# Splitting the aggregation of mixing weights, adding bias on TensorE, and moving two mixes into the first projection

## The reference, cut to what matters

```python
# x: (32, 64, 1024) f32, cond: (32, 128)
h = gelu(cond @ W0 + b0); h = gelu(h @ W1 + b1)
att = softmax(h @ W2 + b2)                       # (32, 8)
agg_w = einsum('bk,koi->boi', att, weight)       # (32, 64, 64)
z = einsum('boi,bih->boh', agg_w, x) + (att @ bias_k)[:, :, None]
# causal self-attention over each batch's 64 rows, 32 heads of 32, with an adapter prefix of 10
x = x + attention(z, w_attn, w_proj, adapter_wte, gating)
x = x + ffn(grouped_conv(x) + cond @ c_weight.T + fside)   # base matmul, router, top-2 LoRA
```

## Time and profile before

| | |
|---|---|
| median of 3 runs | 1165.27 us (1162.61 to 1166.54) |
| the profiled execution | 1160.39 us |
| its span, first to last instruction | 1158.6 us |
| TensorE (PE) busy | 1141.3 us, 99% |
| VectorE (DVE) busy | 926.9 us, 80% |
| ScalarE (ACT) busy | 442.2 us, 38% |

### The profile page before, as it was taken

One profiled execution on the slowest core, in us unless ns is written; L12 is line 12 of the kernel. 1 busy time (PEld: TensorE's weight loads), 2 busy tenths in 40 slices (PEclk: granted clock), 3 DMA queues, 4 the chain that ended last, 5 costly groups with the idle time before them and its releaser, 6 DMA issues.

```text
span 1158.6 us, 19585 instructions
## 1 busy us (share of the span) xinstructions
PE 1141.3 (99%) x7595; PEld 964.7 (83%) x7595; DVE 926.9 (80%) x1742; ACT 442.2 (38%) x815; POOL 55.2 (5%) x25
## 2 busy tenths in 40 slices
PE   6999999999999999999999999999999999999998
PEld 5988888888888888888888888878888888888887
DVE  5987877877877887887887789887867777877775
ACT  4444454453453553553653644423222212122110
POOL 1000000000000000000000000010000022221112
PEclk9999999999999999999999999999999999999999
DMA  8414124124124033133042188776457933434312
GB/s 260 136 55 136 30 91 137 29 91 137 29 94 134 29 107 121 29 121 108 28 133 96 28 294 319 297 210 195 162 184 286 367 104 98 110 115 114 96 37 91
DMA packets 99577, 151.63 MB, mean 131 GB/s; under 512 B 7306, under 2 KB 84126, under 8 KB 96798
## 3 DMA queue, kind: packets, MB, share of 16 engines
q1 hardware_dynamic: 98478, 135.70, 36.6%
q10 hardware_dynamic: 1008, 14.68, 3.1%
HBM read 95.82 MB, written 54.54 MB: 130 GB/s over the span
## 4 chain that ended last, share of the span: by engine, by line
PE 96%; DVE 2%; issue 1%; ACT 0%; DMA 0%; DVEq 0%; ACTq 0%
PE psum L929 45%; PE psum L1001 25%; PE psum L1019 5%; PE psum L881 3%; PE psum L912 3%; PE psum L897 2%; PE psum L1053 2%; PE psum L260 2%; PE psum L1035 2%; PE psum L941 2%; PE psum L950 1%; PE psum L890 1%; PE psum L1037 1%; PE psum L906 1%; DVE z L353 1%
## 5 line engine op out<-in xcount | busy, mean ns | idle before, releaser
L929 PE MATMUL psum<-z,w_hi 128*128 128x512 f32 x1536 | 480.9, 394 | 0.0
L929 PEld LDWEIGHTS psum<-z,w_hi 128*128 128x128 f32 x1536 | 282.5, 188 | 55.0
L929 PE MATMUL psum<-z,w_lo 128*128 128x512 f32 x768 | 299.9, 391 | 0.0
L1001 PE MATMUL psum<-f_wform,f_act_hi 128*128 128x512 f32 (+1 forms) x912 | 279.7, 389 | 2.6 <-DVE f_act_lo L1455 1.8
L1001 PEld LDWEIGHTS psum<-f_wform,f_act_hi 128*128 128x128 f32 x912 | 167.9, 188 | 36.4 <-DVE f_act_lo L1455 2.3
L1001 PE MATMUL psum<-f_wform,f_act_lo 128*128 128x512 f32 (+1 forms) x456 | 176.0, 386 | 0.0
L1221 ACT ACTIVATE a_kbd<-a_kr 32x512 f32<-32x512 f32 x128 | 80.7, 630 | 234.2 <-DVE a_kr L1358 233.0
L929 PEld LDWEIGHTS psum<-z,w_lo 128*128 128x128 f32 x768 | 144.2, 188 | 30.8
L1001 PEld LDWEIGHTS psum<-f_wform,f_act_lo 128*128 128x128 f32 x456 | 85.7, 188 | 17.6
L855 POOL TENSOR_TENSOR f_xn<-f_x,_bbase 128x1024 f32<-128x1024 f32 x16 | 50.4, 3152 | 1026.4 <-DVE f_x L1505 696.2
L1191 ACT ACTIVATE f_act_hi<-f_act_sum 128x512 fp32r<-128x512 f32 x64 | 40.3, 632 | 118.0 <-DVE f_act_sum L1449 45.3
(11 more groups left out here) (176 smaller groups left out, 1564.9 us busy)
## 6 DMA issues: line engine op xcount, KB each, us to landing
w_forms<-f_prep_lo SPq DMA_DIRECT2D x16, 896.0 KB, 4.7
f_wform<-w_forms SPq DMA_DIRECT2D x7, 2048.0 KB, 12.9
f_wform<-w_forms ACTq DMA_DIRECT2D x7, 2048.0 KB, 17.3
w_st<-in_wqkvT SPq DMA_DIRECT2D x7, 1536.0 KB, 7.0
w_forms<-f_prep_hi SPq DMA_DIRECT2D x16, 640.0 KB, 5.8
m_x<-in_x SPq DMA_DIRECT2D x16, 512.0 KB, 4.2
y_scratch<-a_ysb SPq DMA_DIRECT2D x32, 256.0 KB, 2.6
f_raw<-y_scratch SPq DMA_DIRECT2D x8, 1024.0 KB, 5.9
```

The lines of the kernel that those rows point to most:

```text
L929: mm = pe.matmul(dst, w[:, c, x, :], zs, start=(c == 0 and i == 0), stop=(c == KC - 1 and i == 2))
L1001: mm = pe.matmul((prod_bank[i], bank[0])[part][:, cols], a[:, c, :], wform[i][:, w, c, cols], start=(i < 4 and c == 0 and n == 0), stop=(c ...
```

## The change

1. The aggregation is cut in two: `aggregate(0, 4)` in the front, `aggregate(4, 16)` on PE behind mix 3. The copies of the first part come directly behind it, ahead of the split of the K weights; those of the second part are all on ScalarE, behind `high(3)`. Its q=1 bank is now bank 3.
2. For pairs 0 to 5 (`NPE`) the bias is added in PSUM: `bias_raw` holds att × bias_k, an 8-row product per batch; `bias_hl` its fp32r high part (rows 0 to 7) and low part (rows 32 to 39); two fp32r matmuls of 512 columns with a stationary matrix of ones (`bias_ones`) end each such mix. L251, its diagonal and its copy are gone.
3. For these pairs `add` does nothing; `high` and `low` read PSUM (odd pairs in two halves), and a mix that reuses their slot waits for `z_lo`, not for `z_sum`.
4. `AHEAD` goes from 6 to 4: pairs 4 and 5 are mixed in K's first slots, every later pair two slots later; the last, 15, lies behind V's last chunk. The lists of ScalarE and VectorE are rearranged to match.

The diff's core:

```diff
 MIX_COLS = (OB * NC, P // NM)
 DMA_RING = 1024
+NPE = 6
...
+    def slot_parts(i):
+
+        if i % 2 == 0:
+            return ((slice(0, KC), psum[:, 0:1024].rearrange("p (c t) -> p c t", t=P)),)
+        return [(slice(4 * half, 4 * half + 4), slot_bank(i, half).rearrange("p (c t) -> p c t", t=P)) for half in range(2)]
...
+            Tensor.aggregate(pe, *HALVES[0])
+
+        def aggregate(pe, i0, i1):
 
             for n in range(OB):
...
-                    mm = pe.matmul(agg_psum[n // 2][NC * b:NC * (b + 1), 256 * (n % 2):256 * (n % 2 + 1)],
-                                   mixw[:, n * NC:(n + 1) * NC], att_sel[:, b, :, :].rearrange("p o i -> p (o i)"),
-                                   start=True, stop=True)
+                    mm = pe.matmul(agg_psum[n // 2][NC * b:NC * (b + 1), 256 * (n % 2):256 * (n % 2 + 1)]
+                                   .rearrange("p (o i) -> p o i", i=NP)[:, :, i0:i1],
+                                   mixw[:, n * NC:(n + 1) * NC], att_sel[:, b, :, i0:i1], start=True, stop=True)
                 if n % 2:
                     mm.then_inc(agg_mm, 1)
-            pe.wait_ge(aggb_spread, 1)
-            pe.wait_ge(ctx_set, 1)
-            pe.matmul(turned_bank[:], ones[:], aggb_diag[:].rearrange("p b o -> p (b o)"), start=True, stop=True
-                      ).then_inc(aggb_wide, 1)
 
...
             for q in range(2):
                 pe.wait_ge(agg_copied[q], 2 if i < UP else 4)
             pe.wait_ge(x_in[i % NX], 16 * (i // NX + 1))
-            wait(pe, z_sum, i - 1)
+            if 2 <= i < NPE + 2:
+                pe.wait_ge(z_lo, i - 1)
+            elif i >= 2:
+                pe.wait_ge(z_sum, i - 1 - NPE)
             for c in range(KC):
                 mm = pe.matmul(slot_bank(i, c // 4)[:, (c % 4) * P:(c % 4 + 1) * P], xbuf[i % NX][:, c * P:(c + 1) * P],
-                               aggT[:, i, :, :].rearrange("p b o -> p (b o)"), start=True, stop=True)
+                               aggT[:, i, :, :].rearrange("p b o -> p (b o)"), start=c % 4 == 0 or i >= NPE, stop=i >= NPE,
+                               skip_group_check=True)
+            if i < NPE:
+                run = sum(2 * i >= r1 for _, r1 in BIAS_RUNS) + 1
+                pe.wait_ge(bias_hi, run)
+                pe.wait_ge(bias_lo, run)
+                for half in range(2):
+                    mm = pe.matmul(slot_bank(i, half).rearrange("p (c t) -> p c t", t=P), bias_ones[:],
+                                   bias_hl[:, 2 * i:2 * i + 2, :].rearrange("p (a b) o -> p a (b o)", a=1)
+                                   .broadcast_to([LO_ROWS + NM, KC // 2, P]),
+                                   start=False, stop=True, skip_group_check=True)
             mm.then_inc(z_mm, 1)
...
-            act.wait_ge(aggb_spread, 1)
             act.activation(aggb_rows[:], small_bank[0:NB, 256:256 + NC], ACT.Copy).then_inc(aggb_copied, 1)
+            Scalar.agg(act, 0, 0)
+            act.wait_ge(bias_cleared, 2)
+            for n, (r0, r1) in enumerate(BIAS_RUNS):
+                act.wait_ge(bias_raw_set, n + 1)
+                act.activation(bias_hl[0:NM, r0:r1, :], bias_raw[n][:], ACT.Copy).then_inc(bias_hi, 1)
             Scalar.weight_hi(act, K_)
-            act.wait_ge(agg_mm, 1)
+
+        def agg(act, half, q):
+
+            act.wait_ge(agg_mm, 2 * half + q + 1)
             act.wait_ge(cleared, 1)
-            for i0, i1 in HALVES:
-                for b in range(2):
-                    agg_copy(lambda o, i: act.activation(o, i, ACT.Copy), 0, b, i0, i1).then_inc(agg_copied[0], 1)
-                if i0 == 0:
...
+            for b in range(2):
+                agg_copy(lambda o, i: act.activation(o, i, ACT.Copy), q, b, *HALVES[half]).then_inc(agg_copied[q], 1)
...
         def high(act, i):
-            act.wait_ge(z_sum, i + 1)
-            act.activation(z_place(z, i, 0), raw_place(i), ACT.Copy).then_inc(z_hi, 1)
+            if i >= NPE:
+                act.wait_ge(z_sum, i + 1 - NPE)
+                act.activation(z_place(z, i, 0), raw_place(i), ACT.Copy).then_inc(z_hi, 1)
+                return
+            act.wait_ge(z_mm, i + 1)
+            for chunks, src in slot_parts(i):
+                cp = act.activation(z_place(z, i, 0)[:, chunks, :], src, ACT.Copy)
+            cp.then_inc(z_hi, 1)
...
-            dve.wait_ge(aggb_mm, 1)
-            dve.tensor_tensor(aggb_diag[:],
-                              small_bank[0:UB, 256:256 + NC].rearrange("p (a o) -> p a o", a=1).broadcast_to([UB, UB, NC]),
-                              ident[0:UB, 0:UB].rearrange("p (b a) -> p b a", a=1).broadcast_to([UB, UB, NC]), ALU.mult
-                              ).then_inc(aggb_spread, 1)
+            for n, (r0, r1) in enumerate(BIAS_RUNS):
+                if n == 1:
+                    dve.wait_ge(agg_mm, 2)
+                    dve.wait_ge(cleared, 1)
+                    for b in range(2):
+                        agg_copy(dve.tensor_copy, 1, b, *HALVES[0]).then_inc(agg_copied[1], 1)
+                dve.tensor_tensor(bias_raw[n][:],
+                                  attT[:, r0:r1].rearrange("p (b a) -> p b a", a=1).broadcast_to([NM, r1 - r0, NC]),
+                                  biask[:].rearrange("p (a o) -> p a o", a=1).broadcast_to([NM, r1 - r0, NC]), ALU.mult
+                                  ).then_inc(bias_raw_set, 1)
+            dve.wait_ge(bias_cleared, 2)
+            for n, (r0, r1) in enumerate(BIAS_RUNS):
...
+                dve.wait_ge(bias_raw_set, n + 1)
+                dve.wait_ge(bias_hi, n + 1)
+                dve.tensor_tensor(bias_hl[LO_ROWS:LO_ROWS + NM, r0:r1, :], bias_raw[n][:], bias_hl[0:NM, r0:r1, :].bitcast(F32),
+                                  ALU.subtract).then_inc(bias_lo, 1)
...
-            dve.wait_ge(agg_mm, 2)
-            dve.wait_ge(cleared, 1)
-            for i0, i1 in HALVES:
-                for b in range(2):
-                    agg_copy(dve.tensor_copy, 1, b, i0, i1).then_inc(agg_copied[1], 1)
...
+            if i < NPE:
+                return
...
+            if i >= NPE:
+                dve.tensor_tensor(z_place(z, i, 1), raw_place(i), z_place(z_f, i, 0), ALU.subtract).then_inc(z_lo, 1)
+                return
+            for chunks, src in slot_parts(i):
+                low = dve.tensor_tensor(z_place(z, i, 1)[:, chunks, :], src, z_place(z_f, i, 0)[:, chunks, :], ALU.subtract)
+            low.then_inc(z_lo, 1)
...
-            pool.wait_ge(z_sum, 2 * UP)
+            pool.wait_ge(z_sum, 2 * UP - NPE)
...
-                AHEAD = UP + 2
+                AHEAD = UP
                 for i in range(AHEAD):
                     mix_tensor.mix(pe, i)
+                mix_tensor.aggregate(pe, UP, NP)
...
             for i in range(UP):
                 mix_scalar.high(act, i)
+            mix_scalar.agg(act, 1, 0)
+            mix_scalar.agg(act, 1, 1)
             mix_scalar.weight_hi(act, Q_)
...
-            for i in range(UP + 3, NP - 5):
+            for i in range(UP + 3, UP + 5):
...
-                    for i in range(NP - 5, NP - 2):
+                    for i in range(UP + 5, NP - 3):
...
-                    mix_scalar.high(act, NP - 2)
+                    mix_scalar.high(act, NP - 3)
...
+                    mix_scalar.high(act, NP - 2)
...
-            mix_vector.add(dve, 0)
-            for i in range(1, UP):
-                mix_vector.add(dve, i)
-                mix_vector.low(dve, i - 1)
-            mix_vector.low(dve, UP - 1)
-            mix_vector.add(dve, UP)
+            for i in range(UP):
+                mix_vector.low(dve, i)
...
-                    mix_on(UP + 1, UP + 2)
+                    mix_on(UP + 1, UP + 3)
                     mix_vector.weight_lo(dve, Q_)
-                    mix_on(UP + 2, UP + 4)
+                    mix_on(UP + 3, UP + 4)
                     mix_vector.weight_lo(dve, V_)
-                    mix_on(UP + 4, NP - 5)
+                    mix_on(UP + 4, UP + 5)
...
-                    mix_on(NP - 5, NP - 1)
+                    mix_on(UP + 5, NP - 2)
...
-                    mix_on(NP - 1, NP)
+                    mix_on(NP - 2, NP)
```

More of the change, by code:

```diff
@@ L69 @@
 DMA_RING = 1024
+NPE = 6
+BIAS_RUNS = ((0, UB), (UB, 2 * NPE))
+LO_ROWS = 32
 def wait(eng, sem, value):
@@ L106, in mixing @@
     wst, whi, wlo, whi_f, w_first, w_hi, w_lo = first_weights
-    tiny_at, small_at, aggT_at, x_at, aggb_at = places
+    tiny_at, small_at, aggT_at, x_at, aggb_at, bias_at, bias_hl_at = places
     bank = [psum[:, 512 * i:512 * (i + 1)] for i in range(8)]
-    small_bank, turned_bank, agg_psum = bank[7], bank[3], bank[5:7]
+    small_bank, turned_bank, agg_psum = bank[7], bank[3], (bank[5], bank[3])
     def sem(name):
@@ L139, in mixing @@
     xbuf = [Space(nc, "m", at).take(f"x{j}", [P, L]) for j, at in enumerate(x_at)]
-    aggb = [Space(nc, "m", at).take(f"aggb{u}", [P, UT]) for u, at in enumerate(aggb_at)]
```

(35 more changed lines are left out.)

1 line of the change is left out of this document (removed).

## The result

The changed kernel takes 1169.82 us (median of 15), the kernel before 1162.94 on the same chips: ratio 1.0055, interval 1.0043 to 1.0067, slower by 6.4 us. The forecast was +0.27% with a range that holds the time; the likeliest chance was given to "within 0.3%", and it came out slower by more. Three executions among all these measurements, none of the changed kernel itself, ran in a slow state at 1429 us or more and are left out of the ratios. The profiled execution took 1170.39 us, span 1168.6.

A forecast was written before the change was run, and what follows sets the result against it. TensorE bounds the kernel, busy 1141.3 of 1158.6 us. Earlier projection −5.3, moved mixes +4.5, stalls at mixes 4 and 7 +1.95, longer scores wait +2.4, less 0.4: +3.1, 1168.4 us (+0.27%); range 1163.5 to 1171.5.

The forecast's parts named there:

- M: Front, start of mix 0 on PE: forecast at 11.4 us instead of 13.67.
- S: Start of the K projection on PE: forecast at 23.45 us instead of 28.74, 5.3 us earlier.
- the gap: Before the scores at the end of the first unit: PE waits 3.5 us for VectorE's chain, against 1.1 before.
- I have bounds: 0.055 a pass ... I take 1.4: Front, first part of the split aggregation: 16 passes of 64 columns, between 0.9 and 1.8 us, taken as 1.4.
- Rival 2: Both aggregation parts: each pass still costs 0.22 us despite fewer columns; +5.7 us in all, 1171.0; chance 0.12.
- Mix 0 at 1.78 us: Front: 16 mix passes of 128 columns take 1.78 us on PE, before the bias matmuls.
- 2 × 0.23 = 0.45 us more: Mixes of pairs 0 to 5: two fp32r bias matmuls of 512 columns add 0.45 us of PE time each.
- Rival 3: Gap before the scores: the clock drops to 1.2 GHz during unit 1's K projection, 5.5 us more, 1174; chance 0.03.
- Rival 1: Mixes 4, 7 and scores: DVE and ACT keep up, no stalls; scores at 64.9, −2.3 us, 1163.0; chance 0.15.
- The DMA steps: Front loads: transfers move ahead by 1 to 2 us, the wait for x5 disappears, x2 comes in time.
- PSUM as source: VectorE parts read from PSUM: no slower than from SBUF; by the skill's 62-cycle rule, S about 0.2 us longer.
- The profiled execution as base: Forecast time: the +3.1 us derived from one execution of 1160.39 us, added to the median 1165.27 of three runs.

The follow-up runs named there:

- Experiments 6: The changed kernel with low(5) ahead of add(6) on VectorE, nothing else; 1167.24 us in a single execution.
- 1: The changed kernel with low parts 12, 13 and 14 moved behind avs on VectorE, adds left in place; ratio 1.0032, median 1166.05 us.
- 7: The changed kernel with mixes 4 and 5 put back ahead of the K projection, all engine lists as in the kernel before; 1169.42 us, single execution.
- experiment 4: The changed kernel with useless matmuls in PE's idle stretches of the front; ratio 1.0065.
- x5 earlier: The kernel before with the load of x5 directly behind x4's, ratio 0.9971; a second version adds useless matmuls in the front, ratio 0.9983.
- the one with two additions: The kernel before with two useless VectorE additions ahead of avs in unit 0; 1167.18 us in a single execution.
- experiment 5: The changed kernel with bias matmuls over all 128 rows, 1167.21 us, and separately without its bias matmuls, 1164.95 us; single executions.
- three additions: The kernel before with three useless VectorE additions ahead of avs in unit 0; ratio 1.0031, median 1166.63 us.
- experiment 2: The kernel before with useless VectorE additions ahead of avs in unit 0: three, median 1166.63 us, and two, 1167.18 us.
- experiment 3: The kernel before, unchanged, profiled a second time; 1162.76 us.

## Why the prediction was right and wrong

*The order of events* was right throughout. M 11.21 (11.4 forecast); from S to mix 4 2.02 us (2.05); a wait put down to `low` before mix 7 of 1.21 (1.3); from mix 7 to mix 13's signal 22.94 (22.95); from there to the scores 10.08 (10.06); the gap 3.03 (3.5). Mix 4 started when ScalarE's last copy of `aggT` ended (27.93), as costed. Experiments 6 and 1, and 7 by its gap of 1.12 us, show that the order of VectorE's list causes the two waits. One count was wrong: the adds left are 15 rows, not 18.

*"I have bounds: 0.055 a pass ... I take 1.4".* The aggregation took 1.12, and its second part 1.52 where 2.65 was the lower bound. The row of 3.53 us, from which the bounds of the second part came, had itself run slow: 0.22 us for 256 columns against 0.095 for 192 (0.13 for 256 by proportion); the first part fell from 1.12 to 0.69 when PE was kept busy ahead of it (experiment 4). Rival 2 is refuted: with runs of 4 and 12 columns a pass took 0.07 and 0.095 us, not 0.22. The Trainium skill says that a non-contiguous pattern slows matmuls significantly (PSUM — Partial Sum Buffer, Specifications); no such slowing shows in these passes.

*Mix 0 at 1.78 us.* It took 3.66: the step that failed first. In the shown profile of the kernel before, PE's slow start fell on the aggregation, and mixing came behind it. The change took this work away, and mix 0 met the slow array instead. +1.9 us at S. It took 3.4 us or more in all six profiles with this front. But the profile of before was kind here too: in three of six profiles with the old front (both of x5 earlier, and the one with two additions) mix 0 was slow as well.

*"2 × 0.23 = 0.45 us more"* per biased mix: mis-sized, 0.87 measured (experiment 5). The price was taken from rows with 128 rows on both sides. It made the round in the front 2.64 us, set by PE (+0.8 at S), and mixes 4 and 5 dearer (+0.9). So S came at 26.01 instead of 23.45. Together −0.2 + 1.9 + 0.8 + 0.9 = 3.4, the whole difference between 70.3 and 73.7.

*Rival 3, given 0.03, happened.* "Against it, the clock is 1.00 in the front with its gaps" was a reading of gaps of at most 2.49 us; the forecast gap was longer than all of them, and it alone should have raised the chance. It cost 2.8 us by the second mark, not 5.5, since the lower level ended within K; in the five other profiles with a fall at this place (three additions, experiments 4, 5 twice, 6) it cost 1.6. The Trainium skill, TensorE: Matmul & The Clock Gate, section on why this matters for kernels, advises against idle gaps between bursts; experiment 2 agrees, the clock fell behind its gap of 3.31 us.

*Rival 1* fell: no wait was covered. *The DMA steps* held: the front of the changed kernel had no wait for x4 or x5. *PSUM as source*: `low` took 1.22 us for 1024 columns from PSUM (L401), `high` 1.02, as costed.

*The profiled execution as base.* The sum from profile to profile is 6.6 + 2.8 + 0.7 = 10.0 us, where 3.1 was forecast. Between the medians it is 6.9 (6.4 by the ratio), because the profile of before lay 2.6 us under its median and that of the changed kernel 0.6 above. So nearly half of what was missed cancelled. The range was also laid around 1165.27, the median of three executions; that of fifteen is 1162.94. Laid around this one, the range would have ended at 1169.2, and 1169.82 lies outside. The order of events was foreseen; that the time was inside is luck. Why the other executions of the kernel before split into groups near 1162 and near 1165.5 is not shown: the one of experiment 3 had both falls of the clock and took 1162.76.

## What to carry to other kernels

Before filling a stretch that waits, ask which engine's list ends last in the unit and count that list from its last trigger: work moved behind an engine's last instruction starts the other engine's chain late by as much. A gap on TensorE can have a second price behind it, here 1.6 to 2.8 us; a long one is worth breaking up. A single profile can be a lucky one: compare it with the median, and with a second profile, before building on its rows. Look up whether a wait belongs to the engine that the profile names; here the transfer behind it was the cheap thing to mend.

## What the runs showed of the hardware

- Gaps on PE and the granted clock behind them, by place. Before the scores: 0.50 behind 3.03 (five profiles) and 3.31 us, 1.00 behind 2.58, 1.67 and all shorter ones. Before mix 5: 0.50 behind 2.67 and 3.21, 1.00 behind 2.49 and 2.85. Before mix 4: 0.50 behind 2.99. At the wait for `f_act_lo` near 760 us it fell in six of fourteen profiles, behind 1.83 to 2.14 us, and stayed at 1.00 in eight, behind the same lengths; the kernel before did both (1.83 stayed, 1.85 fell). Length alone does not decide.
- Behind one and the same gap of 3.03 us the scores took 2.25 us in the changed kernel and 1.24 with 128 rows, where the lower level began only behind them.
- The view of the granted clock says 1.00 from the start, but equal instructions take twice as long at first: 16 passes of a mix 3.66 us at 11 us, 1.88 when PE had been busy since 5.7 (experiment 4). When this ends differs between executions of equal work: L251 took 1.12, 1.47 and 2.07 us, and in three profiles mix 0 of the old front, at about 15 us, was still slow. With only two useless matmuls ahead L244 stayed at 3.68.
- Two fp32r matmuls over 40 rows between matmuls over 128 cost 0.39 us more than the same over 128 rows with zeros (4.11 against 3.72 us from mix 4 to mix 5).
